# Macaron layer with sparse experts on one core: rows scattered by expert, plain block reads, one-step SiLU, low parts on VectorE

## The reference

```python
x = x + 0.5 * ffn(layernorm(x))
x = x + attn(layernorm(x))
x = x + 0.5 * ffn(layernorm(x))

def ffn(x):                                   # 4096 tokens of 256
    probs = softmax(x @ gate_w.T)             # 8 experts
    weights, indices = top_k(probs, 2); weights /= weights.sum(-1)
    h = silu(x @ w_gate[e]) * (x @ w_up[e])   # per expert e, 176 wide
    out = sum over the two experts of  weight * (h @ w_down[e])
    sh = silu(x @ shw_gate) * (x @ shw_up) @ shw_down      # 352 wide
    return out + sigmoid(x @ shgate_w) * sh

def attn(x):                                  # 16 heads of 16
    q, k = rope(x @ Wq), rope(x @ Wk); v = x @ Wv
    b = clip(sigmoid(x @ Wg + bg), 0.8, 0.9995)
    S = S * b_t + phi(k_t) v_t ;  z = z * b_t + phi(k_t)   # phi = elu + 1
    y_t = phi(q_t) S / (phi(q_t) z + eps)
    return y @ Wo + bo
```

## Time and profile before

| | us |
|---|---|
| median of 3 runs | 1254.88 (1252.7 to 1256.25) |
| profiled execution, span from first to last instruction | 1247.3 |
| PE busy | 1013.0 (81%) |
| DVE busy | 791.5 (63%) |
| POOL busy | 659.9 (53%) |
| ACT busy | 478.9 (38%) |
| mean granted TensorE clock | 0.865 |

### The profile page before, as it was taken

The page is one execution under the profiler, slowest core; times in us unless marked ns, Lnnn a source line. Parts: engine busy times, 40 slices in busy tenths (PEclk is TensorE's granted clock), DMA queues, the critical chain, the costliest instruction groups (busy, mean ns, idle before and its releaser), DMA issues.

```text
span 1247.3 us, 22940 instructions
## 1 busy us (share of the span) xinstructions
PE 1013.0 (81%) x6928; PEld 923.9 (74%) x6928; DVE 791.5 (63%) x2299; ACT 478.9 (38%) x1303; POOL 659.9 (53%) x758
## 2 busy tenths in 40 slices
PE   2745978499999659999999999977756899996674
PEld 2745877489999538888888888777745799995674
DVE  4335756356676557888888865545653567664675
ACT  3223332145555324445445544222321355552111
POOL 3646656244443445667767735245663444443884
PEclk9866889689999868899999989778857899998877
DMA  7584435034434210000000001055660244342433
GB/s 224 30 136 68 20 18 18 5 109 124 123 120 111 64 37 20 27 27 24 29 27 27 18 2 35 1 18 21 31 35 3 86 123 124 119 122 77 141 102 119
DMA packets 63733, 79.92 MB, mean 64 GB/s; under 512 B 12352, under 2 KB 54816, under 8 KB 63616
## 3 DMA queue, kind: packets, MB, share of 16 engines
q1 hardware_dynamic: 46336, 42.83, 20.0%
q0 software_dynamic: 17280, 35.62, 11.4%
HBM read 46.88 MB, written 31.52 MB: 63 GB/s over the span
## 4 chain that ended last, share of the span: by engine, by line
PE 50%; POOL 14%; DVE 11%; issue 10%; DMA 7%; DVEq 2%; ACT 2%; another core or an unknown queue 1%; SPq 0%; POOLq 0%; ACTq 0%
PE PSA L1447 13%; PE PSA L1548 7%; POOL MEM L897 5%; PE PSA L1499 4%; POOL tokens L846 4%; PE PSA L1465 4%; POOL MEMR L862 3%; PE PSA L1430 3%; PE PSA L1455 3%; PE PSA L1374 2%; DMA tokens<-CN,POSU 2%; DVEq L1076 2%; DVE X L1274 2%; PE PSA L1403 2%; PE PSA L1519 2%
## 5 line engine op out<-in xcount | busy, mean ns | idle before, releaser
L876 POOL DMA_INDIRECT MEM<-normed,SLOT x142 | 134.9, 950 | 164.1 <-PE PSA L1430 156.6
L1388 PE MATMUL PSA<-MEMR,SGUh 128*128 128x256 f32 (+1 forms) x768 | 185.5, 325 | 8.8 <-DVE MEM L1164 6.2
L1447 PE MATMUL PSA<-EGUh,MEMR 128*128 x568 | 177.0, 353 | 3.5 <-issue 2.0
L1403 PE MATMUL PSA<-SDh,MEMR 128*128 128x256 f32 (+1 forms) x384 | 105.9, 339 | 78.3 <-POOL MEMR L862 71.2
L897 POOL DMA_INDIRECT MEM<-expert_out,POSU x128 | 124.4, 972 | 53.8 <-issue 28.7
L1388 PEld LDWEIGHTS PSA<-MEMR,SGUh 128*128 128x128 f32 (+1 forms) x768 | 147.6, 221 | 6.9 <-DVE MEM L1164 6.4
L846 POOL DMA_INDIRECT tokens<-CN,POSU x128 | 124.7, 974 | 43.9 <-issue 32.1
L1403 PEld LDWEIGHTS PSA<-SDh,MEMR 128*128 128x128 f32 (+1 forms) x384 | 82.7, 239 | 83.5 <-POOL MEMR L862 58.9
L976 ACT ACTIVATE MEM<-PSA 128x256 f32<-128x256 f32 (+1 forms) x96 | 36.5, 380 | 245.0 <-POOL MEMR L862 136.1
L1548 PEld LDWEIGHTS PSA<-MEM 128*128 128x128 f32 x1024 | 125.7, 199 | 1.5 <-DVE MEM L1324 1.5
L1548 PE MATMUL PSA<-MEM 128*128 128x18 f32 x1024 | 124.6, 265 | 1.1 <-DVE MEM L1324 1.1
(11 more groups left out here) (174 smaller groups left out, 2584.9 us busy)
## 6 DMA issues: line engine op xcount, KB each, us to landing
expert_out<-MEM SPq DMA_DIRECT2D x142, 128.0 KB, 1.7
normed<-MEM SPq DMA_DIRECT2D x16, 512.0 KB
X<-in_L_attn_x SPq DMA_DIRECT2D x8, 512.0 KB, 7.7
out<-X SPq DMA_DIRECT2D x8, 512.0 KB, 4.1
MEM<-normed,SLOT POOLq DMA_INDIRECT x142
tokens<-CN,POSU POOLq DMA_INDIRECT x128
MEM<-expert_out,POSU POOLq DMA_INDIRECT x128, 2.8
MEM<-in_L_ffn_w_gate SPq DMA_DIRECT2D x8, 176.0 KB, 8.2
```

What stands on the lines that cost most here:

```text
L876: pool.indirect_dma_start(out=XG[j % 4], out_offset=None, in_=xn_d[f], in_offset=bass.IndirectOffsetOnAxis(ap=SLOT[:, j:j + 1], axis=0)).t ...
L1388: last = mm(t[0:h, w * HALF:(w + 1) * HALF], SGU[b][:, w, k, j * P:j * P + h], XT[slot][a][:, k, hf * HALF:(hf + 1) * HALF], start=i == 0, ...
L1403: last = mm(t[:, c * D:(c + 1) * D], (HH, HL)[a][m % 3][0:h, c * P:(c + 1) * P], SD[b][0:h, j, :], start=j == 0 and i == 0 and c == 0, sto ...
L1447: last = mm(t[:, 0:2 * HE], XGR[j % 2][a][:, k, :], EGU[b][:, bass.ds(e, 1), k, :], start=i == 0, stop=i == 3 * KD - 1)
```

## The change

1. **Rows, not numbers, are scattered.** `XN` gets two more columns (`RW = D + 2 = 258`): the first expert's number and twice the token's number. POOL scatters whole rows of 1032 bytes to `expert_rows`, a DRAM region with 4096 + 128 rows per expert, with as many scatters as before (64 per FFN). The plain store of the normalised rows, the lists and their gather, transpose and cast go.
2. **Fetches are plain.** A slot's 128 rows are now consecutive, so SP reads them as one block at a row number that it loads from `SRC`. Rows behind each expert's end must hold fillers: SP writes 7 fixed blocks and 8 at the experts' ends (`slots` on SP), from a tile that POOL makes in a new step `blank`, which stands behind the last scatters.
3. **Results are scattered, reads are plain.** POOL computes each row's place from the two extra columns (`YIDX`, L884) and scatters the 128 result rows to `2 * token + k` (L889, 71 per FFN, in place of SP's plain store). `collect` becomes one plain SP read of 128 x 512 per tile.
4. **One-step SiLU.** ACT computes Silu itself, and DVE's `(tanh + 1) * gate` and the drain behind it go, in shared units and in expert slots. The top-2 weights use tanh in place of exp.
5. **All low parts of the shared expert are made by DVE** (`low_on` is always "dve").
6. **Tiles go round the four batches**: tile `n` is chunk `n // 4` of batch `n % 4`, so that a state update needs the one of four chunks before. Loads and stores of `X` follow; their runs stay 1 KB.

```diff
-        self.units, self.units_by, self.low, self.low_on = 0, {}, [], "pool"
+        self.units, self.units_by, self.low, self.low_on = 0, {}, [], "dve"
@@ table
         for s in self.route(f, NG - 1)[5:]:
             s()
+        self.add("blank", f)
         self.take(("count", f))
...
-        self.take(("lines", f))
-        self.add("lines", f)
...
-            if n % CB != CB - 1:
+            if n < NT - B:
@@ sync
-            def scale(r, half):
...
-                    sp.dma_start(dst, XN[n.xn]).then_inc(s_xst[n.xn], 16)
-
-            def expert_down(f, j):
-                taken(sp, ("y", f, j))
-                sp.dma_start(y_d[f][j * P:(j + 1) * P, :], YS[j % 3]).then_inc(s_ys[j % 3], 16)
+            def slots(f):
+                sp.wait_ge(s_blank, f + 1)
+                for w in range(E - 1):
+                    sp.dma_start(rows_d[f][E * ES + w * P:E * ES + (w + 1) * P, :], FILL[:, E + w:E + w + RW]).then_inc(s_fill, 16)
+                sp.wait_ge(s_ends, f + 1)
+                ends = [sp.value_load(NEI[0:1, e:e + 1], min_val=e * ES, max_val=e * ES + ROWS) for e in range(E)]
+                for e, end in enumerate(ends):
+                    sp.dma_start(rows_d[f][bass.ds(end, P), :], FILL[:, e:e + RW]).then_inc(s_fill, 16)
+
+            def fetch(f, j):
+                if j == 0:
+                    sp.wait_ge(s_slots, f + 1)
+                    sp.wait_ge(s_fill, 16 * PADS * (f + 1))
+                    for k in range(3):
+                        sp.wait_ge(s_xst[k], stored(f_end(f), k))
+                    sp.wait_ge(s_dn, plan.units_by[f])
...
+                if j >= 4:
+                    ready(sp, ("xg", f, j - 4))
+                    sp.wait_ge(s_yidx, f * SLOTS + j - 3)
+                row = sp.value_load(SRC[0:1, j:j + 1], min_val=0, max_val=E * ES + (E - 2) * P)
+                sp.dma_start(XG[j % 4], rows_d[f][bass.ds(row, P), :]).then_inc(s_fetch[j % 4], 16)
+
+            def collect(f, i):
...
+                sp.dma_start((YG1, YG2)[f][i % ring], y_view[f][:, i, :]).then_inc(s_yg[f][i % ring], 16)
@@ gpsimd
+                i = n.g * GT + c
                 for k in range(2):
-                    i = n.g * GT + c
-                    pool.indirect_dma_start(out=id_d[n.f], out_offset=bass.IndirectOffsetOnAxis(ap=POSU[:, k, i:i + 1], axis=0),
-                                            in_=tok[:, i:i + 1], in_offset=None).then_inc(s_sct, 16)
+                    pool.indirect_dma_start(out=rows_d[n.f], out_offset=bass.IndirectOffsetOnAxis(ap=POSU[:, k, i:i + 1], axis=0),
+                                            in_=XN[n.xn][:, c, :], in_offset=None).then_inc(s_xst[n.xn], 16)
...
-                pool.indirect_dma_start(out=XG[j % 4], out_offset=None, in_=xn_d[f],
-                                        in_offset=bass.IndirectOffsetOnAxis(ap=SLOT[:, j:j + 1], axis=0)).then_inc(s_fetch[j % 4], 16)
+            def expert_x(f, j):
...
+                nc.gpsimd.tensor_scalar(YIDX[:, j % 8:j % 8 + 1], x[:, D:D + 1], EJ[:, j:j + 1], x[:, D + 1:D + 2], ALU.is_equal, ALU.add).then_inc(s_yidx, 1)
+
+            def expert_down(f, j):
+                taken(pool, ("y", f, j))
+                pool.wait_ge(s_yidx, f * SLOTS + j + 1)
+                pool.indirect_dma_start(out=y_d[f], out_offset=bass.IndirectOffsetOnAxis(ap=YIDX[:, j % 8:j % 8 + 1], axis=0),
+                                        in_=YS[j % 3], in_offset=None).then_inc(s_ys[j % 3], 16)
-            def collect(f, i):
...
-                for k in range(2):
-                    pool.indirect_dma_start(out=got[k], out_offset=None, in_=y_d[f],
-                                            in_offset=bass.IndirectOffsetOnAxis(ap=POSU[:, k, i:i + 1], axis=0)).then_inc(s_yg[f][i % ring], 16)
@@ scalar, vector
-                a(TH[m % 2][0:h, :], t[0:h, 0:HALF], ACT.Tanh, scale=0.5).then_inc(s_th, 1)
+                a(TH[m % 2][0:h, :], t[0:h, 0:HALF], ACT.Silu).then_inc(s_th, 1)
...
-                v.scalar_tensor_tensor(TH[m % 2][0:h, :], TH[m % 2][0:h, :], 1.0, t[0:h, 0:HALF], ALU.add, ALU.mult)
-                settle()
```

302 lines of the change are left out of this document (129 added, 173 removed).

## The result

| | before | after |
|---|---|---|
| median, us | 1255.57 (4 runs, 1252.7 to 1259.66) | 1113.88 (4 runs, 1103.11 to 1119.83) |
| ratio, 95% interval | | 0.8903 (0.8789 to 0.9017) |
| profiled execution, span | 1247.3 | 1101.3 |
| PE, DVE, POOL busy | 81%, 63%, 53% | 86%, 66%, 50% |

A forecast was written before the change was run, and what follows sets the result against it. PE was taken to bound attention and experts, POOL the tail and scatter-bound feed groups, a scatter's landing the table. Gains 19 (tail) + 22 (tables) + 30 (feeds) - 2 (attention) = 69 gave 1178 profiled, 1186 median; range 1150 to 1235.

The forecast's parts named there:

- Feeds, 30 of 60 us: Both feeds: moving low parts off POOL and the SiLU edit gain 30 us of PE's 60 us idle time.
- I take half: Feeds: between ends of 0 and 60 us, weight arrival and the router's chain hide part, so the gain is 30.
- the congestion lifts: Rival, feeds: 4-byte scatters and 512 KB stores slowed transfers, so all 60 us of idle go; 1156 us, chance 0.17.
- Experts, 0: Experts of both FFNs: the change gains nothing, because PE sets the time.
- PE sets 2.29 us per slot: Experts: PE, busy 159 of 162.5 us per FFN, bounds each of 71 slots, so nothing is gained.
- Tail, 19: Tail: 64 POOL gathers become 32 plain SP reads; DVE and PE are next, about 74 us, gain 19 us.
- the block of 8.2 us: Tail: DVE's time for a group of four tiles and three units; eight of them make 66 us.
- neither hides the other: Tail: DVE's 66 us and PE's 65.35 us are close and overlap only partly, so 74 us was taken.
- Table, 11 per FFN: Table stages: first rows 27.7 us after the row numbers (T) rather than 38.9, gain 11 us per FFN, 22 in all.
- Attention and its start, -2: Attention: nothing gained; three more table loads at 1.28 us cost 2 us, ends 0 and 4.
- The slower rivals: Row scatters at the slow rate in the feeds, 1262 us, chance 0.09; experts' results landing late, +383 us, chance 0.05.
- 1262's side: Time if row scatters ran at 0.33 us per row, lengthening the feeds: 1186 + 76 us, chance 0.09.

The follow-up runs named there:

- e4: The kernel before, its 4-byte scatters replaced by as many scatters of 1 KB rows of constants, with a fixed token list; 1190.22 us, ratio 0.946.
- e11: The kernel before, its 4-byte scatters replaced by as many scatters of 64-byte rows, with a fixed token list; 1199.92 us, ratio 0.938.
- e14: The changed kernel itself, unaltered, measured again on another chip; 1138.46 us, ratio 0.906.
- e12: The kernel before with 1 KB scatters of constants and all low parts on VectorE, two-step SiLU kept; 1212.77 us, ratio 0.947.
- e6: The changed kernel with the two-step SiLU put back everywhere; 1166.37 us, ratio 0.928.
- e7: The changed kernel with the shared expert's low parts back on POOL outside the table stages; 1125.52 us, ratio 0.897.
- e1: The kernel before with the one-step SiLU alone, and top-2 weights from tanh; 1260.65 us, ratio 0.991.
- e10: The kernel before with one-step SiLU, experts' rows fetched by plain SP reads of fixed tiles in place of POOL's gathers; 1273.07 us, ratio 0.993.
- e8: The changed kernel with filler tile, counts and slot table made before the last group's scatters, so fillers run beside them; 1089.93 us, ratio 0.869.
- e5: The kernel before with 1 KB scatters of constants, one-step SiLU and all low parts on VectorE; 1142.14 us, ratio 0.910.

## Why the prediction was wrong

- **Feeds, 30 of 60 us: the step that failed first.** The step is "I take half": the arrival of weights and the router's chain were taken to hide half of the gain. Measured 59.7, the size of all of PE's idle time (though 9 us of idle time remain in 742 to 810 us), and the rival "the congestion lifts" had the mechanism, its evidence (0.33 us per 1 KB row at the earlier trace rows against 0.061 at the earlier trace rows) and the size of 60; it got 0.17. The argument against it, the router's chain, cost nothing. The arrival of weights was itself a victim of the 4-byte scatters, as e4 and e11 show. But the 4-byte scatters are 42 of the 59.7 us (35.2 + 6.5, e4); the other 18 came with SiLU and low parts, so that the rival's 60 fits this well is in part luck. The unnamed waits of the earlier trace rows are gone in e4, e11 and after, but e14 has such waits without any 4-byte item, so these are not explained by them alone.
- **SiLU and low parts in the feeds**: the forecast counted VectorE's 0.42 for 0.41 us and took POOL's relief as the gain. By e12 the relief alone gains nothing; e6 shows that the one-step SiLU is worth 13 and 12 us in the feeds of after, and e7 that the place of the low parts is worth 7 and 3.
- **Experts, 0: "PE sets 2.29 us per slot" was wrong.** Measured 12 us per FFN, slot 2.01. A busy share of 98% was read as a bound, and with it falls the sentence ahead of the prediction that such a stage can't be made shorter by work on other engines. The same row had PEld busy 146.95 of 162.5, and after has 143.92 of 147: the weight loads showed the idle time that modelled ends of matmuls had filled. e6 shows that the two-step SiLU alone brings the loss back, e1 that removing it alone gives 3 of the 12 us. Which of the moves of fetch and result the other 9 need besides is open (e10).
- **Tail, 19.** Measured 36.8 with its start and end. DVE is the bound, which was the lower end of the term (66 us); the block of 8.2 us was too long: by the starts shown above a group takes 2.20 + 2 x 0.96 + 3 x 0.84 + 0.97 = 7.6 us, and 58.6 / 8 = 7.3 on average. More than half of the difference is the pair of combines, 2.20 for 2.56 us: the 2.56 were read in the earlier trace rows where POOL's subtraction held the first of the four up to 0.95 us, and the prediction took POOL's work away without taking that away. The rest is that a product and a low part follow each other by 0.84 and not 0.92 us. PE's clock rose, 0.94 for 0.77, and its 50.5 us hide beside DVE's 50.45; the 74 us that stood for "neither hides the other" were 8 too many over DVE's 66. The first `combine` came earlier, not later: a result's scatter is followed by one plain read rather than two gathers. That this is the reason is argued.
- **Table, 11 per FFN.** Measured 8.3 and 7.7, rows at T + 30.5 rather than T + 27.7. The queue order was as described; `blank` came 1 us later than counted; from SP's seventh filler to its eighth, with the register loads between, went 5.3 us rather than 3.6; the first seven fillers took 0.52 us each in place of 0.42; from the last filler's issue to the first fetch it was 3.5 us rather than 2.5; and the first fetch with its landing took 2.2 us rather than 3.7. But e4 puts the term in another light: with fast transfers the old chain takes 27.5 us, 3 less than the new one. The wait that the change removes was long only because of the 4-byte items, and the wait that it adds is the dearer one, until e8 takes it off the path.
- **Attention and its start, -2.** Measured 9.4 us, two thirds of it at the start, where e5 still has 36.7 and after, e6, e7 and e8 have 32 to 33: it came with the reads on SP or with the new order of the tiles, which no run separates. The three more table loads are there (four in after, one in before, 1.28 us each). The rest is within the clock's play.
- **The slower rivals.** Row scatters didn't run at the slow rate: from 125 to 178 us of after they cost 0.197 x 16 x 53 us for 3.70 MB, 3585 rows, 0.047 us each, less than the gathers' 0.061; and results landed in time: PE, ACT and DVE never waited for one in the experts. The 6 pieces of a row that the prediction allowed for cannot occur either: 1032 bytes from a multiple of 8 touch five blocks of 256 bytes, never six. The row, from the DMA queues:

```profile
q0 software_dynamic: 1344, 3.70, 19.7%
```

- **The range.** It reached to 1262's side, where nothing happened, and ended below at 1150, one rival's case with the other terms at their middle. The better ends of all its own terms, 27 + 30 + 60, would have given 1138, below that range. Feeds and tail came at or beyond their better ends together, and the experts' term had no range at all, because a busy share had been taken for a bound.

## What to carry to other kernels

Before giving the gain of a faster transfer a cover, ask what sets the cover: a queue of 4-byte indirect writes made the stores, the weight loads and so the whole first stage slow, and the sign was in one row, a high DMA share at a low rate. A PE share near 100% is not yet a bound: look whether the weight loads are as busy (90% and 98% in the experts before and after) and whether slot times alternate (2.0, 2.3). This is a sign and no proof: in the attention PEld is busy 85% of the time, and no run made it shorter. Two edits that use the same engine's time must be priced together and beside the bottleneck that stands: with 4-byte scatters SiLU gave 1% and both edits a loss of 2 to 3%; once these were gone, both gave 19 us in the feeds and 15 in the tail (e5 against e4). And when one engine is relieved, price its neighbour's instructions anew.
